# Two routed adapter layers: the order of work on four engine queues is changed

## The reference

```python
h = x @ W_down[kind] + b_down[kind]          # 1024 -> 512
h = gelu(h)
u = h @ W_up[kind] + b_up[kind]              # 512 -> 1024
y = x + u
y = (y - mean(y)) * rsqrt(var(y) + 1e-5)     # over the 1024
x = y * gamma[kind] + beta[kind]
```

## Time and profile before

| | |
|---|---|
| median of 3 runs | 2715.4 us (2714.55 to 2716.41) |
| profiled execution, its own time | 2714.55 us |
| its span, first to last instruction | 2712.7 us |
| PE busy | 2673.8 us, 99% |
| DVE, ACT, POOL busy | 73%, 61%, 44% |
| DMA | 573 MB, mean 211 GB/s |
| mean granted TensorE clock | 0.998 |

### The profile page before, as it was taken

How to read it: one execution, slowest core, us unless ns; L and a number is a source line. 1 busy time by engine, 2 the same in 40 slices (tenths; PEclk the granted TensorE clock), 3 DMA queues, 4 the chain that set the end, 5 groups by cost and what they waited for, 6 DMA issues and landing times.

```text
span 2712.7 us, 54420 instructions
## 1 busy us (share of the span) xinstructions
PE 2673.8 (99%) x11720; PEld 2197.9 (81%) x11720; DVE 1989.2 (73%) x3360; ACT 1660.2 (61%) x2906; POOL 1187.9 (44%) x1050
## 2 busy tenths in 40 slices
PE   8999999999999999999999999999999999999997
PEld 6888888887788888888878888888878888888885
DVE  6666666678767666666797777777887777777776
ACT  5666665666666566566666656656665665665665
POOL 1445444445544444444434434444334444444445
PEclk9999999999999999999999999999999999999999
DMA  6656666666665665666877666666777666666664
GB/s 228 216 189 221 207 202 213 209 229 233 231 211 198 203 223 196 214 208 200 259 215 219 197 218 204 203 216 202 249 217 225 200 211 200 214 209 207 206 203 152
DMA packets 360737, 573.36 MB, mean 211 GB/s; under 512 B 40162, under 2 KB 239970, under 8 KB 359394
## 3 DMA queue, kind: packets, MB, share of 16 engines
q1 hardware_dynamic: 358850, 554.14, 63.6%
q10 hardware_dynamic: 1440, 15.47, 1.6%
HBM read 364.97 MB, written 204.47 MB: 210 GB/s over the span
## 4 chain that ended last, share of the span: by engine, by line
PE 93%; DVE 4%; issue 2%; DMA 1%; DVEq 0%; ACT 0%; ACTq 0%; SPq 0%
PE pD L537 49%; PE bX L549 25%; PE bZ L549 19%; DVE wul L907 1%; DVE wdl L888 0%; DMA rwu<-in_Wu 0%; DVE xt L1015 0%; DVE hl L997 0%; DVE xt L1038 0%; DVE hT L982 0%; DVE xl L975 0%; DVE xt L1007 0%; DMA xt<-in_itok 0%; DMA xq<-in_xB 0%; DVE cbu L922 0%
## 5 line engine op out<-in xcount | busy, mean ns | idle before, releaser
L478 POOL TENSOR_TENSOR xt<-xt,cgb 128x1024 f32<-128x1024 f32 x258 | 627.2, 2432 | 707.9 <-ACT xt L729 707.9
L537 PE MATMUL pD<-wdh,xh 128*128 128x512 f32 x2080 | 810.4, 390 | 6.2 <-DVE xl L975 4.2
L537 PE MATMUL pD<-wdh,xl 128*128 128x512 f32 x2080 | 809.9, 389 | 0.0
L537 PE MATMUL pD<-wdl,xh 128*128 128x512 f32 x2080 | 809.9, 389 | 0.0
L729 ACT ACTIVATE xt<-xt,rstd 128x1024 f32<-128x1024 f32 x258 | 296.7, 1150 | 274.0 <-DVE xt L1038 256.3
L537 PEld LDWEIGHTS pD<-wdh,xh 128*128 128x128 f32 x2080 | 390.8, 188 | 90.3 <-DVE xl L975 5.0
L721 ACT ACTIVATE pC<-xt,nmean 128x512 f32<-128x512 f32 x520 | 357.4, 687 | 169.4 <-DVE nmean L1023 156.6
L537 PEld LDWEIGHTS pD<-wdh,xl 128*128 128x128 f32 x2080 | 390.8, 188 | 81.5
L537 PEld LDWEIGHTS pD<-wdl,xh 128*128 128x128 f32 x2080 | 390.7, 188 | 80.9
L486 POOL TENSOR_TENSOR cs<-hT 128x256 f32<-128x256 f32 x130 | 98.5, 758 | 785.4 <-DVE hT L982 762.9
L711 ACT ACTIVATE hh<-cs 128x512 fp32r<-128x512 f32 x260 | 163.0, 627 | 436.6 <-PE bX L549 359.5
(11 more groups left out here) (119 smaller groups left out, 3625.0 us busy)
## 6 DMA issues: line engine op xcount, KB each, us to landing
xq<-in_xB SPq DMA_DIRECT2D x130, 512.0 KB, 3.3
htok<-hg SPq DMA_DIRECT2D x260, 256.0 KB, 2.1
hq<-htok SPq DMA_DIRECT2D x1040, 64.0 KB, 3.6
xt<-in_x SPq DMA_DIRECT2D x130, 512.0 KB, 5.2
mid<-xt SPq DMA_DIRECT2D x130, 512.0 KB, 3.4
xq<-mid SPq DMA_DIRECT2D x520, 128.0 KB, 3.0
xt<-mid SPq DMA_DIRECT2D x130, 512.0 KB, 6.0
out<-xt SPq DMA_DIRECT2D x128, 512.0 KB, 3.2
```

Of the source, the lines that this page charges most:

```text
L478: eng.tensor_tensor(xt[:, k, :], xt[:, k, :], cgb[:, 1, :], ALU.add).then_inc(s_o, 1)
L537: last = eng.matmul(pD[e][:, :], a[:, e, 128 * k:128 * k + 128], w[:, k, :], start=False, stop=(k == 7 and n == 2), skip_group_check=True)
```

## The change

No instruction is added or taken out, and PE's stream is as before. Inside the hand-written orders of SP, POOL, ACT and DVE, calls change places:

- SP: the second half of `load_h` goes ahead of `load_rows`, `store(z, 0)` ahead of `store_h(i, 0)`, and `gains` and `up_biases` to the end of the step.
- POOL: `sums(w)` goes ahead of the wait for new gains and of the token `s_cg`.
- ACT: `high_h(i-2, 0)` goes behind `gelu` and `seed_d`; the weight loads go to the start of `end`; `take_wu_0` and `high_x` go ahead of `normal` and `gelu`; `high_h(w, 2)` ahead of `seed_d`; `seed_z` ahead of the squares; two squares ahead of `high_h(w, 3)` and `take_wd_1`.
- DVE: `onto` 1 becomes the first instruction of `begin`; `variance` goes behind `onto` 3; `low_h(w, 0)` ahead of `onto` 3 and `take_wu_2`; `transpose_x(i+1, 0)` behind `last_onto` 4; in `end`, `take_wd_0` and `low_h(w, 1)` go first, `transpose_x(i+1, 1)` and `low_h(w, 2)` behind them, and `last_onto` 7, `mean` and `take_wu_1` after that.

```diff
--- before.py
+++ after.py
@@ -408,22 +408,22 @@
 
             def step(i):
                 u, v, w, z = i + -3, i + -1, i + -2, i + -4
+                kinds.read(i + 1)
                 load_h(v, 0)
                 store_h(v, 1)
                 if not (i + 1).first():
                     load_blocks(i + 1, 1)
+                load_h(v, 1)
                 load_rows(w, 0)
                 load_rows(w, 1)
-                kinds.read(i + 1)
-                if i.first():
-                    up_biases(i)
-                load_h(v, 1)
+                store(z, 0)
                 store_h(i, 0)
-                store(z, 0)
-                kinds.when_new(u, gains)
                 if not (i + 1).first():
                     load_blocks(i + 2, 0)
                 store(z, 1)
+                kinds.when_new(u, gains)
+                if i.first():
+                    up_biases(i)
                 if not v.first():
                     kinds.when_new(v, up_biases)
 
@@ -492,11 +492,11 @@
 
             def step(i):
                 w, z = i + -2, i + -4
+                sums(w)
                 if z.exists():
                     kinds.read(z)
                     kinds.when_new(z, take_gb)
                     eng.sem_inc(s_cg, 1)
-                sums(w)
                 norm(z)
                 shift(z, 0)
                 shift(z, 1)
@@ -747,49 +747,49 @@
                 kinds.read(i + 2)
                 if not i.first():
                     high_x(i, 1)
-                high_h(i + -2, 0)
                 gelu(i + -1, 1)
+                if not i.first():
+                    seed_d(i, 1)
                 if (i + -2).first():
                     take_wu_2(Pair(0))
+                high_h(i + -2, 0)
                 if i.first():
                     fetch_up(eng, adapter(i), 0)
                 if not (i + -3).first():
                     kinds.when_new(i + -3, take_wu_2)
-                if not i.first():
-                    seed_d(i, 1)
 
             def end(i):
                 u, w = i + -3, i + -2
                 if not (i + 1).first():
                     kinds.when_new(i + 1, load_bias)
+                kinds.when_near(w, load_up)
+                kinds.when_far(i, load_up)
+                kinds.when_near(i + 1, load_down)
+                kinds.when_far(i + 2, load_down)
                 high_h(w, 1)
-                kinds.when_near(w, load_up)
+                if not w.first():
+                    kinds.when_new(w, take_wu_0)
                 normal(u + -1, 0)
-                gelu(i, 0)
                 if not (i + 1).first():
                     high_x(i + 1, 0)
-                if not w.first():
-                    kinds.when_new(w, take_wu_0)
+                gelu(i, 0)
+                high_h(w, 2)
                 if not (i + 1).first():
                     seed_d(i + 1, 0)
                 normal(u + -1, 1)
                 if not (i + 1).first():
                     kinds.when_new(i + 1, take_wd_0)
-                high_h(w, 2)
                 seed_x(w)
-                kinds.when_far(i, load_up)
+                seed_z(w)
                 square(u, 0, 0)
-                kinds.when_near(i + 1, load_down)
-                kinds.when_far(i + 2, load_down)
+                square(u, 0, 1)
                 high_h(w, 3)
+                if not (i + 1).first():
+                    kinds.when_new(i + 1, take_wd_1)
+                square(u, 1, 0)
+                square(u, 1, 1)
                 if (i + -1).first():
                     take_wu_0(Pair(0))
-                if not (i + 1).first():
-                    kinds.when_new(i + 1, take_wd_1)
-                seed_z(w)
-                square(u, 0, 1)
-                square(u, 1, 0)
-                square(u, 1, 1)
 
             steps(eng, halves(begin, end), -1, NPH + 5, 0, 5, 5)
 
@@ -1071,45 +1071,45 @@
                 if (u + -1).last():
                     last_rows(u + -1)
                     return
+                onto(u, 1, X, 0, 0)
                 if not i.first():
                     kinds.when_new(i, take_wd_1)
                 ready(i, s_wd[1])
+                if u.first():
+                    take_wu_6(Pair(0))
                 transpose_h(w, 0)
                 transpose_h(w, 1)
-                onto(u, 1, X, 0, 0)
-                if u.last():
-                    variance(u + -1)
-                if not u.last():
-                    variance(u + -1)
                 if not i.first():
                     low_x(i, 1)
-                onto(u, 2, bZ, 1, 1)
-                onto(u, 3, X, 0, 1)
-                if u.first():
-                    take_wu_6(Pair(0))
                 if (i + -1).first():
                     factors(Pair(0))
-                transpose_x(i + 1, 0)
                 if (i + -2).first():
                     take_wu_1(Pair(0))
                 kinds.read(i + 1)
+                onto(u, 2, bZ, 1, 1)
+                low_h(w, 0)
+                if u.last():
+                    variance(u + -1)
+                onto(u, 3, X, 0, 1)
                 if not u.first():
                     kinds.when_new(u, take_wu_2)
-                low_h(w, 0)
                 ready(u, s_wu[2])
+                kinds.when_near(w, factors)
+                if not u.last():
+                    variance(u + -1)
+                if only_up(i):
+                    low_h(w, 1)
                 scale(u + -1, 0)
                 scale(u + -1, 1)
-                kinds.when_near(w, factors)
-                if only_up(i):
-                    low_h(w, 1)
                 last_onto(u, 4, bZ, 0, 1, 3)
+                transpose_x(i + 1, 0)
                 last_onto(u, 5, X, 1, 1, 2)
-                if not (i + 1).first():
-                    low_x(i + 1, 0)
                 if not w.first():
                     kinds.when_new(w, take_wu_0)
                     ready(w, s_cb)
                 ready(w, s_wu[0])
+                if not (i + 1).first():
+                    low_x(i + 1, 0)
                 last_onto(u, 6, bZ, 0, 0, 1)
                 mean(u, 0, 6)
 
@@ -1117,25 +1117,26 @@
                 u, w = i + -3, i + -2
                 if (u + -1).last():
                     return
-                transpose_x(i + 1, 1)
-                if w.first():
-                    take_wu_4(Pair(0))
-                kinds.when_far(i + -1, factors)
                 if not (i + 1).first():
                     kinds.when_new(i + 1, take_wd_0)
                 ready(i + 1, s_wd[0])
+
+                if not only_up(i):
+                    low_h(w, 1)
+                transpose_x(i + 1, 1)
+                low_h(w, 2)
+                if w.first():
+                    take_wu_4(Pair(0))
                 last_onto(u, 7, bX[u.c % 2], 1, 0, None)
+                mean(u, 1, 7)
+                kinds.when_far(i + -1, factors)
                 if not w.first():
                     kinds.when_new(w, take_wu_1)
-                if not only_up(i):
-                    low_h(w, 1)
-                mean(u, 1, 7)
-                low_h(w, 2)
                 ready(w, s_wu[1])
+                low_h(w, 3)
                 if (i + -1).first():
                     take_wu_0(Pair(0))
                     ready(Pair(0), s_cb)
-                low_h(w, 3)
 
             steps(eng, halves(begin, end), -1, NPH + 5, 1, 4, 4)
 
```

## The result

The changed kernel took 2742.96 us (median of 4 runs, 2742.49 to 2745.17), the kernel before 2714.98 beside it: a ratio of 1.0102, 95% interval 1.0089 to 1.0114. The forecast was 2710.0. The profiled execution took 2742.87 us with a span of 2741.1.

The account below looks back on a forecast made before the run. TensorE was taken as the bound (PE busy 99%, at most 60 us to win, only in short stretches). Terms -1.1-1.5-2.2-2.6+2.0 = -5.4 us gave 2710.0 from the median of 2715.4; own range 2707.5 to 2713.5, chance 0.50.

Parts of the forecast that it names:

- Calm steps, 0: Steps away from switches: nothing lost or won, as the smallest slack of what TensorE waits for is 2.6 us.
- Loop edges, -1.1: Every sixth step: `onto` 1 ahead of the transposes ends ten delays of product 2; -1.1 us, bounds 0 to -1.1.
- First stall of a switch, -1.5: Switched pair's own step: `onto` 1 first removes layer 0's stall, partly layer 1's; -1.5 us, bounds +0.5 to -3.9.
- The group two steps on, -2.2: Stalls two steps after a switch: work leaving DVE's chain before `take_wu_2` shortens product 4's wait; -2.2 us, bounds 0 to -4.
- Head, -2.6: Start of kernel: later `cbu` load and earlier bias seed shorten two PE waits; -2.6 us, bounds 0 to -4.6.
- The 1.0 for `cbu`: Head's first wait: issuing the 512 KB of `cbu` later wins 1.0 us, between nothing and 2.3; PE resumes at 39.15.
- Drain, +2.0: Last steps: transposes, POOL's sums and `scale` come later, so product 5 waits longer; +2.0 us, bounds +0.5 to +3.5.
- calm steps lose their slack: Rival, every step: `scale` waits for POOL's sums, slowed beside DVE, making `last_onto` 4 late; 2723 us, chance 0.08.

Follow-up runs that it names:

- b_onto1: Kernel before with one move: DVE's `onto` 1 ahead of the down half's weight splits and the transposes of h; 2714.58 us.
- a_end: Kernel after with the second half of DVE's step put back in the order of before; 2729.90 us.
- b_best: Kernel before with `onto` 1 first except in the drain's steps, and ACT's bias seed of the second down half earlier; 2709.32 us.
- b_best_tx: Kernel before with `onto` 1 first outside the drain, the early bias seed, and the first transpose of x behind `last_onto` 4; 2707.66 us.
- b_pool: Kernel before with POOL's new order alone; 2714.39 us.
- b_dve: Kernel before with DVE's whole new order alone; 2731.21 us.
- a_onto1back: Kernel after with one move undone: the transposes of h again ahead of `onto` 1; 2761.21 us.
- b_act: Kernel before with ACT's new order alone; 2729.93 us.
- b_wu0: Kernel before with ACT's four weight casts of a switch moved ahead of `normal`, the high part of x and gelu; 2730.61 us.
- b_wu0_s64: Kernel before with ACT's four weight casts moved up and POOL's `shift` cut to 64 of 1024 columns; 2729.76 us.
- b_shift64: Kernel before with POOL's `shift` cut to 64 of 1024 columns, the rest of the offset left out; 2718.59 us.

## Why the prediction was wrong

- **Calm steps, 0:** right. 20.40 us a step. But most of DVE's 211 us lie in them, about 1.5 us a step (462.11 against 417.21 us busy from 700 to 1320), and it was hidden: the slack had been worked out as 2.6 us or more.
- **Loop edges, -1.1:** -0.4 in the whole change; -1.6 in b_onto1, where the move stood alone.
- **First stall of a switch, -1.5:** measured +6.8, outside the bounds. A wait before product 3 came in layer 1 as forecast, but at 1.55 and 1.61 (1339.98 and 1968.74) instead of some 1.1, and in layer 0, where none was forecast, at 1.58. With `onto` 1 moved alone it is 0.48 or less. What was missing is in DVE's second half, where the low parts of h now stand ahead of `last_onto` 7, beside `shift`: a_end, which puts them back, has 3.5 us here, 0.5 below before. b_onto1 and b_best have 1.2 and 1.4.
- **The group two steps on, -2.2:** measured +19.0, of which 4.7 are matmuls at the dropped clock. This is the step that failed, and 19.0 of the 27.9 us lie in it. It said "What counts is what leaves the chain before `take_wu_2`" and gave bounds of 0 to -4, with no loss. It took every duration from rows of before, as if an instruction brought its length along to a new neighbour; ACT's move of the weight casts ahead of `normal`, which sets when `shift` runs, was not weighed at all, and `variance` counted only as work that leaves a chain. What the runs showed in its place: lengths changed with the neighbour (the splits and the subtraction 4.4 us longer beside `shift`), and with `shift` cut the groups of the kernel after fall from 31.1 to 16.3. The term that it did compute, the transpose that leaves the chain, shortens product 4's wait in b_best_tx by 0.55 to 0.57 us, and the waits before product 1 take that back.
- **Head, -2.6:** -2.3 measured, near the term partly by luck. The seed's wait is real, and the early seed gives 2.5 us by itself, where the term had some 2; waits at 52.04 and 60.5 take back 1.2, where it had 0.5. The 1.0 for `cbu` is not shown: PE resumed between 37.4 and 40.2 in the 11 kernels whose SP order was that of before (39.0 on average) and between 37.7 and 39.4 in the 9 others (38.5), so one execution's 39.11 says nothing on it.
- **Drain, +2.0:** +4.8. `scale` starts 7.2 us after product 0 instead of 5.2 (1.95 later, where 1.6 was worked out), and product 5 waits 1.1 more, as forecast. But the second step repeated the 1.1 in full instead of 0.4, and some 1.4 is the dropped clock. Of the two causes given for `scale`, POOL's token is wrong: b_pool's drain is unchanged, and b_dve has 12.5 us with the token still ahead of the sums. The other fits: in the kernel after and in b_dve `scale` starts as soon as the `low_h` (2694.28) ends that now stands ahead of it and needs POOL's sums. It is DVE's order.
- **Rivals:** "calm steps lose their slack" had the mechanism, POOL and DVE holding each other up, on the wrong pair (sums and `scale`) and the wrong place (all steps). Its check, four sums at 1.7 us, was made against the calm steps' 2.6 us of slack, and not against the switches, which have none.

What is left open: SP's 5.7 us alone; how the losses divide between the two collisions (low parts of h, weight splits) and the stretched `norm`, since undoing each also moves the other, and the cut of `shift` leaves `norm` stretched (1606 ns); and why product 1's wait in a_end takes the place of product 2's. Which of DVE's other moves costs the drain the rest (a_onto1back still has 10.9 there, 1.4 of it at the dropped clock, against 8.3) was not tried either.

## What to carry to other kernels

An order is also an overlap: before costing a reordering with the durations of the old trace, list for each two-input DVE instruction what POOL will run beside it in the new order, above all in the stages without slack. Bound such a term on the loss side by one length of POOL's neighbour for each meeting (here 2.4 us). And of a reordering of four queues, run each queue alone and then small moves: here three moves taken out of it make 0.3%, where all of them together lose 1.0%.

## What the runs showed of the hardware

- A low part of h on DVE (two SBUF inputs, 0.69 us) that starts during a 2.4 us POOL addition ends about 0.55 us after it, however early it started (104 of 105, begun 0.01 to 2.11 us into it): 0.69 became 2.25. `last_onto`, with one input in PSUM, keeps 0.69 us beside the same instruction. POOL's own short ones suffer the same way beside DVE's splits (1.76 instead of 0.74) and beside `scale`, be they two columns wide (1611 ns instead of 731). POOL's 2.4 us ones barely do (2432 ns on average before, 2443 after).
- The granted clock fell to 0.50 (1.2 GHz) after some stalls of 1.8 us and more, in stretches otherwise at 1.00, nearly each time for 6 to 13 matmuls and 1.1 to 2.6 us lost. After others it stayed, up to 3.15 us (2698.56) and 3.18 (b_dve, 2687.14). Before, with stalls up to 2.07 us, it never fell outside the head; in b_best, b_act, b_wu0, b_wu0_s64 and b_shift64 it fell after the same first stall of the drain (2.04 or 2.05 us). Which of two like stalls drops it stays open.
- Making POOL's `shift` seven times shorter did not make the kernel before faster, but 3.7 us slower, mostly at loop edges. Why is open.
